# A group's sums made half a slot to a slot earlier in the first layer's edge loop

## What is computed

```python
xl = (x @ W_l + b_l).reshape(n, HEADS, C)
xr = (x @ W_r + b_r).reshape(n, HEADS, C)
e = (edge_attr @ W_e).reshape(-1, HEADS, C)
g = leaky_relu(xl[src] + xr[dst] + e, 0.2)
logits = einsum('ehc,hc->eh', g, att)
ex = exp(logits - segment_max(logits, dst)[dst])
alpha = ex / (segment_sum(ex, dst)[dst] + 1e-16)
out = segment_sum(xl[src] * alpha[..., None], dst) + bias
```

## Time and profile before

| | |
|---|---|
| median of 3 runs | 6166.23 us |
| profiled execution | 6159.02 us |
| its span, first to last instruction | 6157.2 us |
| TensorE busy in the span | 4314.0 us (70%) |
| VectorE | 3169.2 us (51%) |
| ScalarE | 1716.0 us (28%) |
| GpSimd | 3265.6 us (53%) |
| mean granted clock of TensorE | 0.741 |

### The profile page before, as it was taken

The page is one execution under the profiler, slowest core; times in us unless marked ns, Lnnn a source line. Parts: engine busy times, 40 slices in busy tenths (PEclk is TensorE's granted clock), DMA queues, the critical chain, the costliest instruction groups (busy, mean ns, idle before and its releaser), DMA issues. The chain is left out here.

```text
span 6157.2 us, 112260 instructions
## 1 busy us (share of the span) xinstructions
PE 4314.0 (70%) x32016; PEld 3566.6 (58%) x32016; DVE 3169.2 (51%) x5361; ACT 1716.0 (28%) x3718; POOL 3265.6 (53%) x3415
## 2 busy tenths in 40 slices
PE   2358888888888888823999955555545555553899
PEld 2336666666666666613999944444444444443899
DVE  8678888888888888737222132222222222223221
ACT  0035555555555555500000002222222222222100
POOL 3647666666666666540000037777777777775000
PEclk9678888888888888855999955555555555555899
DMA  9335555555555555523999924455544455553698
GB/s 361 112 114 161 163 165 164 158 157 162 162 163 161 158 160 161 146 51 106 368 365 365 335 83 150 159 164 162 163 160 156 152 162 163 163 162 103 285 391 327
DMA packets 629300, 1157.89 MB, mean 188 GB/s; under 512 B 163337, under 2 KB 462826, under 8 KB 603428
## 3 DMA queue, kind: packets, MB, share of 16 engines
q1 hardware_dynamic: 380568, 751.54, 34.4%
q10 hardware_dynamic: 139564, 287.74, 14.5%
q0 software_dynamic: 108768, 114.68, 9.1%
HBM read 820.79 MB, written 490.14 MB: 213 GB/s over the span
## 5 line engine op out<-in xcount | busy, mean ns | idle before, releaser
L715 POOL DMA_INDIRECT att_gl<-tab_l,att_ix x1568 | 1503.2, 959 | 735.6 <-issue 471.2
L1239 POOL DMA_INDIRECT sum_gl<-tab_l,sum_ixs x1568 | 1480.2, 944 | 494.9 <-issue 477.6
L962 ACT ACTIVATE att_acc<-att_pc 128x392 bf16<-128x392 f32 x2352 | 1078.5, 497 | 1123.9 <-PE att_pc L737 925.6
L734 PE MATMUL att_pc<-att_ohl,att_ohv 128*128 128x392 bf16 x2352 | 844.3, 359 | 188.6 <-DVE att_ohl L837 188.6
L1159 PE MATMUL sum_pt<-sum_eye,sum_a 128*128 128x128 bf16 x2401 | 309.5, 309 | 930.1 <-ACT sum_at L1175 910.3
L737 PE MATMUL att_pc<-att_acc,att_ohv 128*128 128x392 bf16 x2352 | 839.8, 357 | 116.1 <-ACT att_acc L962 112.4
L1159 PEld LDWEIGHTS sum_pt<-sum_eye,sum_a 128*128 128x128 bf16 x2401 | 223.8, 137 | 994.0 <-ACT sum_at L1175 916.3
L1116 DVE TENSOR_TENSOR sum_t<-sum_pb,sum_gl 128x512 f32<-128x512 f32 x196 | 135.6, 692 | 1237.4 <-DMA sum_gl<-tab_l,sum_ixs 1237.4
L1149 PE MATMUL sum_pb<-sum_wbs,sum_ea 64*128 64x64 f32 x3136 | 719.9, 421 | 30.2 <-DMA sum_ea<-in_ea64P 28.5
L1149 PEld LDWEIGHTS sum_pb<-sum_wbs,sum_ea 64*128 64x128 f32 x3136 | 683.2, 327 | 69.4 <-issue 40.4
L753 PEld LDWEIGHTS att_pl<-att_xe,att_S 128*128 128x128 f32 x3136 | 584.2, 212 | 145.1 <-issue 121.7
(11 more groups left out here) (395 smaller groups left out, 4817.0 us busy)
## 6 DMA issues: line engine op xcount, KB each, us to landing
A<-att_acc SPq DMA_DIRECT2D x2352, 98.0 KB
l_a<-A SPq DMA_DIRECT2D x147, 1568.0 KB, 9.2
att_dall<-in_dst ACTq DMA_DIRECT2D x224, 448.0 KB
hop_at<-AT SPq DMA_DIRECT2D x56, 1568.0 KB, 8.8
sum_a<-A SPq DMA_DIRECT2D x49, 1568.0 KB, 10.6
AT<-sum_at SPq DMA_DIRECT2D x49, 1568.0 KB, 6.5
l_at<-AT SPq DMA_DIRECT2D x42, 1568.0 KB
tot<-att_o ACTq DMA_DIRECT2D x56, 1022.0 KB, 4.1
```

Source lines behind the costliest of these rows:

```text
L715: nc.gpsimd.indirect_dma_start(out=gl[s][:, c, :], out_offset=None, in_=g.tab_l, in_offset=bass.IndirectOffsetOnAxis(ap=ix[s][:, c:c + 1], ...
L734: nc.tensor.matmul(to[:, 0:LO], ohv[c][h][:, m, :, 0], ohl[c][h][:, m // 2, :, m % 2], start=True, stop=False)
L962: nc.scalar.activation(acc[c][n % CR][:, :], pc[(CH * n + c) % CB3][:, 0:LO], ACT.Copy).then_inc(s_acc[c], 1)
L1239: nc.gpsimd.indirect_dma_start(out=gl[q][:, j, :], out_offset=None, in_=g.tab_l, in_offset=bass.IndirectOffsetOnAxis(ap=ixs[q][:, j:j + 1] ...
```

## The change

The sums of batch b move up. Group 0 is made in k = 2 of batch b + 1 (places 3 and 4), groups 1 and 2 in k = 3, and group 3 in k = 0 of batch b + 2. Slot k = 1 has none any more. ScalarE's `keep_sums` goes along, and with group 3's the store. After the loop one group of the last batch but one is left instead of two. No instruction is added or taken out of the whole.

```diff
@@ TensorE, turn(i) @@
+                            if k == 2 and first and m in (3, 4):
+                                sums(b - 1, 1 - s, 0, range(0, 4) if m == 3 else range(4, GQ))
                             if k == 3 and first and m in (0, 1, 3, 4):
-                                sums(b - 1, 1 - s, m // 3, range(0, 4) if m % 3 == 0 else range(4, GQ))
-                            if k < 2 and second and m in (0, 1):
-                                sums(b - 2, s, 2 + k, range(0, 4) if m == 0 else range(4, GQ))
+                                sums(b - 1, 1 - s, 1 + m // 3, range(0, 4) if m % 3 == 0 else range(4, GQ))
+                            if k == 0 and second and m in (0, 1):
+                                sums(b - 2, s, 3, range(0, 4) if m == 0 else range(4, GQ))
 
                 turns(pe, TURNS, turn)
-                for q in (2, 3):
-                    sums(LAST - 1, (LAST - 1) % R, q, range(GQ))
+                sums(LAST - 1, (LAST - 1) % R, 3, range(GQ))
@@ ScalarE, turn(i) @@
+                            if k == 2 and first and m == 5:
+                                keep_sums(b - 1, 1 - s, 0)
                             if k == 3 and first and m in (2, 5):
-                                keep_sums(b - 1, 1 - s, m // 3)
-                            if k < 2 and second and m == 3:
-                                keep_sums(b - 2, s, 2 + k)
+                                keep_sums(b - 1, 1 - s, 1 + m // 3)
+                            if k == 0 and second and m == 3:
+                                keep_sums(b - 2, s, 3)
 
                 turns(act, TURNS, turn)
-                keep_sums(LAST - 1, 0, 2)
                 keep_sums(LAST - 1, 0, 3)
```

## The result

The changed kernel takes 6011.4 us in the median of four runs (5973.7 to 6019.6), the kernel before, beside it on the same chip, 6162.8 (6154.7 to 6169.9): ratio 0.9743 [0.97, 0.9786]. That is 151 us less, where 92 were forecast (6070 us, range 5960 to 6150). The profiled execution took 6012.6 us (span 6010.8, mean granted clock 0.752), 146.4 us less than that of before.

The account below looks back on a forecast made before the run. It took the bound to be a full-clock chain from TensorE's k = 1 through `xb` and VectorE to k = 3, plus a slow slot 7. 27 turns x 3.29 us plus 3 at the tail save 92: 6070 us, range 5960 to 6150.

Parts of the forecast that it names:

- The sum for a turn: Gain for one pass of the loop's body (two batches, slots 0 to 7): 1.27 + 1.61 + 0.85 - 0.44 = 3.29 us.
- L823's wait, 1.61 us: VectorE's wait for group 0's sums at the head of slot 4 goes entirely, 1.61 us a turn; bounds 0 and 1.61.
- The 5.09 us at L823: VectorE's wait at the head of slot 0 goes but merges with its wait for slow slot 7's last matmul; counted nothing.
- `xb`, 1.27 and 0.85 us: VectorE's holes before the messages: slot 2's goes (mean 1.27 us), slot 6's 1.54 us shrinks by 0.85.
- The store, 0.44 us: Store `tot` moved to k = 0 delays ScalarE's next `acc` eviction 0.88 us; counted every second turn, a 0.44 us loss.
- Moved groups in k = 2: Each adds 1.9 us of TensorE, twice a turn; expected covered by existing waits, without waiting for messages; counted nothing.
- a fall of the clock still once a turn: Main forecast's expected sign: TensorE's clock still drops to 0.50 once a turn, some 3 us sooner after the slow slot.
- the clock no longer falls: Rival: slot 7 stays at full clock, saving 6 us a turn, 5908 us in all turns; chance 0.17 for some or all.
- in every second turn: The clock rival's milder form: slot 7 stays at full clock in every second turn, giving 5989 us; within that rival's 0.17.
- turns without a stretch at 0.50: Sign named for the forecast being wrong: turns whose clock never drops to 0.50, with the time then under 6000 us.
- The second fall: Rival: clock also falls before slot 2, costing 6.9 us a turn; 6256 us, or 6160 in every second turn; chance 0.10.
- what ScalarE was to take back: Rival: store delay in both k = 0 slots and evictions in k = 2 lose 2.9 us; 6118 us; chance 0.13 including TensorE.

Follow-up runs that it names:

- e1: Kernel before, sums unmoved, with count matmuls repeated (twelve and five) where TensorE waits in front of slot 7; 6013.2 us, 0.9748 of the kernel before.
- e2: Changed kernel plus count matmuls repeated (seven and five) where TensorE waits in front of slot 7; 5918.8 us, 0.9594 of the kernel before.
- e11: Kernel before with only group 0 moved to k = 2, plus matmuls repeated in front of slots 7 and 4; 5949.6 us, 0.9657 of the kernel before.
- e8: Kernel before with only k = 1 relieved (groups 2 and 3 in k = 0), plus repeated matmuls; 6016.3 us, 0.9773 of the kernel before.
- e5: Changed kernel with the store `tot` issued in k = 3 instead of k = 0, no repeated matmuls; 5975.4 us, 0.9721 of the kernel before.
- e6: Changed kernel with repeated matmuls and the store `tot` in k = 3; 5912.4 us, 0.9606 of the kernel before.
- e9: Changed kernel with repeated matmuls and the store `tot` in k = 2; 5945.6 us, 0.9649 of the kernel before.
- e12: Changed kernel with repeated matmuls and the store `tot` split between slot 3 (s = 0) and slot 6 (s = 1); 5937.3 us, 0.9629 of the kernel before.

## Why the prediction was right, and where not

*What bounds.* Right: the chain through k = 1, `xb`, messages and one-hots, and a slow slot 7 behind a TensorE that idles. e1 and e2 show the second part, as repeats alone keep slot 7 at full clock.

*The sum for a turn,* 3.29 us, came to 2.9 in the turns it was made for. That it is so near is in part luck: without the store it was 3.73, where 2.9 and the store's 1.2 to 1.6 make 4.1 to 4.5. Two errors offset each other. Its terms:

- L823's wait, 1.61 us: the wait for sums went entirely, but 0.32 us of idling stay there, so the hole shrank by 1.3; slot 3 takes 8.4 us where it took 9.8. This is the move that is shown to pay: alone it makes a full-clock turn 2.4 us shorter (e11).
- The 5.09 us at L823 counted nothing where slot 7 is slow, as said: most of it is in the 6.14 us hole at L846. At full clock the same wait is 1.66 us (e1) and does count, which the sum had no term for.
- `xb`, 1.27 and 0.85 us: the holes went, nearly as sized (81.2 - 23.9 = 57 us over 27 turns, 2.1 a turn). That they are worth it is not shown: the relief of k = 1 with a second group in k = 0 brings nothing (e8), and at full clock the whole change, with its store in k = 0, takes no less than group 0's move alone (e2's 71.5 against e11's 71.3 us). No run has the relief alone, without the second group and the store in k = 0.
- The store, 0.44 us, was too small: e5 shows 1.2 to 1.6. I had given slot 4 room that it doesn't have (0.82 us wait of TensorE, slot 4 from 8.3 to 9.1 us).
- Moved groups in k = 2 counted nothing, and no wait of TensorE for messages has come up there.

*The step that failed* is "a fall of the clock still once a turn", taken for 27 turns. It came in 16 of 26. The rival "the clock no longer falls" had the right price, 6 us against 6.2 measured, and "in every second turn", 5989 us, was near the 6011 measured; I gave it, in some or all turns, 0.17. So what came was the rival and not the main case, which is 59 us off, and the sign that I had named for being wrong, turns without a stretch at 0.50, came with it (two with none at all, four with under 1 us). My argument against it, that TensorE would still wait 1.5 us or more, was right as a number (1.47 and 0.97) and did not decide: turns with these waits went both ways. In the timelines the waits in front of slot 7 came to 3.0 to 3.4 us before, where all 26 turns fell, and to 1.8 to 2.5 after; there the turns with the least (1.83 and 1.97) fell, and one with 2.48 did not. So the hole's length alone doesn't say which turn falls. The turns mostly alternate: only twice do two without a fall stand side by side. What else decides I didn't find.

*The other rivals.* The second fall came in two turns of 26, for 3.4 us in slot 5 and in slot 1 and not for a whole slot; they are the longest two of the 26 (79.7 and 79.9 us, 2.3 and 2.4 above the mean of their kind). Of what ScalarE was to take back, the store's 0.88 us in both k = 0 slots nearly came (1.2 to 1.6 us a turn); the evictions in k = 2 don't show, as slots 2 and 6 are no longer than before (8.9 and 9.4 us, before 9.4 and 9.5).

## What to carry to other kernels

Where a clock falls behind a hole, price the hole's shrinking by both outcomes in shares of the turns, not as one or the other; and test it with matmuls repeated into the hole, which takes most of the clock's part out of the comparison and here was worth as much alone as the whole change. A change of two moves may owe what it brings to one of them, so run the halves, and see that a half adds nothing that the whole hasn't. A wait that is hidden behind a slow stretch counts again once that stretch is gone. And before a large store moves, look at what is queued behind it in each place: with the clock up, none of the places tried for this one gave back what it had cost in k = 0.

## What had not been expected of the hardware

With a store of `tot` issued shortly ahead of the end of the loop's body ScalarE's stop there is 3.5 to 4.5 us instead of some 2.5 (e6, and e5 behind the turns that don't fall). Elsewhere late landings of small stores come with it, waited for up to 4.6 us in e9 and 5.3 in e12. Whether the jump back waits for the store's transfer no run shows.

GpSimd may be the next bound. Its gathers follow each other at 1.25 us in e2, with 0.3 us between them for which the profile shows no wait:

```profile
1122.90 0.94 POOL L716 DMA_INDIRECT att_gl<-tab_l,att_ix  x1 [0.31 <-issue]
1124.14 0.95 POOL L716 DMA_INDIRECT att_gl<-tab_l,att_ix  x1 [0.30 <-issue]
```

56 of them make 70.0 us a turn, and e2's shortest turn takes 70.1. Single turns can be shorter, as the gathers are a batch ahead (69.0 us in e5), and in e2 they still wait 30 us in all for messages, so no run here stands at that bound.
